# The norm's guard as a 33rd summed value, and two powers in one operation, in a Mamba scan kernel on one core

## The reference

```python
def _layernorm(x, axis=-1, eps=1e-05):
    ...
    return (x - m) / jnp.sqrt(v + eps)
...
xn = x * jax.lax.rsqrt(var + 1e-06) * norm_w        # a second norm, on the layer norm's result
...
def step(h, inp):                                   # h: 8 batches x 256 channels x 16 states
    dA_t, dB_t, x_t, C_t, t = inp
    h = h * dA_t + dB_t * x_t[:, :, None]
    nrm = jnp.sqrt(jnp.sum(h * h, axis=(1, 2), keepdims=True))
    fac = jnp.minimum(20.0 / (nrm + 1e-08), 1.0)
    h = jnp.where(t % 10 == 0, h * fac, h)
    y = jnp.einsum('bdn,bn->bd', h, C_t) + D_param * x_t
    return (h, y)
```

## Time and profile before

| what | us |
|---|---|
| median of 3 runs | 736.2 |
| lowest and highest of them | 733.01, 736.84 |
| span of the profiled execution | 732.8 |
| PE, DVE busy in it | 610.7, 579.2 |
| ACT, POOL busy in it | 581.7, 591.9 |

### The profile page before, as it was taken

How to read it: one execution, slowest core, us unless ns; L and a number is a source line. 1 busy time by engine, 2 the same in 40 slices (tenths; PEclk the granted TensorE clock), 3 DMA queues, 4 the chain that set the end, 5 groups by cost and what they waited for, 6 DMA issues and landing times.

```text
span 732.8 us, 12812 instructions
## 1 busy us (share of the span) xinstructions
PE 610.7 (83%) x3988; PEld 475.9 (65%) x3988; DVE 579.2 (79%) x918; ACT 581.7 (79%) x1218; POOL 591.9 (81%) x567
## 2 busy tenths in 40 slices
PE   6698989889979889998988999898878794289774
PEld 4346667757757667766766766776667783179764
DVE  5577799899889989998998999889898982843221
ACT  4899989999998999999999999999988731233330
POOL 4488889999998989999998999998798860177774
PEclk9889899999989999999999999999988887589998
DMA  5341423245145313614542271244215202147561
GB/s 159 117 157 36 146 80 117 62 143 162 61 145 144 127 63 100 202 61 133 156 127 63 85 210 64 105 139 133 64 66 175 66 18 73 47 129 207 167 182 48
DMA packets 61735, 83.17 MB, mean 114 GB/s; under 512 B 14998, under 2 KB 47544, under 8 KB 61672
## 3 DMA queue, kind: packets, MB, share of 16 engines
q1 hardware_dynamic: 57896, 76.07, 34.0%
q0 software_dynamic: 2560, 6.08, 3.0%
q10 hardware_dynamic: 1216, 0.27, 0.2%
HBM read 69.81 MB, written 12.80 MB: 113 GB/s over the span
## 4 chain that ended last, share of the span: by engine, by line
ACT 27%; PE 22%; issue 17%; POOL 15%; DVE 13%; DMA 4%; POOLq 0%; SPq 0%; DVEq 0%; ACTq 0%
ACT z L1098 9%; POOL h L855 8%; DVE h L1367 7%; PE ps L1725 7%; ACT ps L989 7%; POOL h L869 4%; PE ps L1617 4%; DMA z<-rows_d,gidx 3%; PE ps L588 2%; PE ps L601 2%; ACT L1059 2%; ACT dtb L1059 1%; ACT xx L1016 1%; PE ps L1699 1%; ACT L1098 1%
## 5 line engine op out<-in xcount | busy, mean ns | idle before, releaser
L1367 DVE TENSOR_TENSOR_SCAN h<-ps,h 128x902 f32<-128x902 f32 x204 | 320.4, 1610 | 33.5 <-ACT ps L989 23.6
L855 POOL TENSOR_TENSOR h<-u,scr 128x640 f32<-128x640 f32 x208 | 298.2, 1462 | 2.4
L1725 PEld LDWEIGHTS ps<-h,ident 128*128 128x128 f32 x1632 | 239.4, 199 | 24.2 <-issue 21.8
L1725 PE MATMUL ps<-h,ident 128*128 128x160 f32 x1632 | 243.9, 310 | 3.3 <-issue 3.3
L1098 ACT ACTIVATE z<-dtb,asc 128x240 f32<-128x240 f32 x576 | 237.4, 485 | 0.3
L989 ACT ACTIVATE ps<-z 128x820 f32<-128x820 f32 (+1 forms) x208 | 138.2, 689 | 16.0 <-DVE h L1367 8.9
L869 POOL TENSOR_TENSOR h<-h,scr 128x960 f32<-128x960 f32 (+1 forms) x52 | 106.0, 2038 | 1.1 <-DVE h L1383 1.1
L1418 DVE TENSOR_TENSOR h<-h,ps 128x640 f32<-128x640 f32 (+2 forms) x169 | 106.5, 642 | 0.2
L1617 PE MATMUL ps<-xnT,wT 128*128 128x488 f32 x144 | 77.2, 652 | 0.3 <-ACT xnT L974 0.3
L1699 PE MATMUL ps<-sqb,sel 128*8 128x32 f32 x832 | 33.6, 195 | 37.6 <-ACT sqb L999 27.7
L1699 PEld LDWEIGHTS ps<-sqb,sel 128*8 128x8 f32 x832 | 27.2, 91 | 53.0 <-ACT sqb L999 45.7
(11 more groups left out here) (193 smaller groups left out, 820.2 us busy)
## 6 DMA issues: line engine op xcount, KB each, us to landing
scr<-b_d SPq DMA_DIRECT2D x52, 640.0 KB, 4.6
scr<-c_d SPq DMA_DIRECT2D x52, 240.0 KB, 4.4
z<-in_L_ffn_w_dram SPq DMA_DIRECT2D x32, 256.0 KB, 3.1
cdg<-cdg_d SPq DMA_DIRECT2D x52, 93.8 KB, 2.1
xx_d<-xx SPq DMA_DIRECT2D x8, 256.0 KB, 2.0
xxr<-xx_d SPq DMA_DIRECT2D x8, 256.0 KB, 2.8
rows_d<-h2b SPq DMA_DIRECT2D x16, 120.0 KB, 2.0
rows_d<-xxr SPq DMA_DIRECT2D x16, 120.0 KB, 2.3
```

What stands on the lines that cost most here:

```text
L855: pool.tensor_tensor(o.rearrange("p (n b) t -> p n b t", b=B), us.unsqueeze(1).to_broadcast([P, nn, B, SEG]), bb[:, S % RING, n0 * BS:(n0 ...
L1367: dve.tensor_tensor_scan(hs, region(G)[:, 0:(r1 - r0) * SLOT], hs, 0.0, ALU.mult, ALU.add).then_inc(gscan, 1)
L1725: pe.matmul(ps[:, YB, 0:H * BS], ident[:], hr[:, :, n * B:(n + 1) * B, 0:SEG], start=(n == 0), stop=False)
```

## The change

The guard that POOL added becomes a 33rd value of each batch in `sqb`. It is written once at the start, and PE and DVE sum 33 values where they summed 32. `root` is the power alone, and the semaphore `nrt_done` between its two operations goes. In `ln_pool` the two powers of 4 values each become one of 8, and the product that gives `nmean` moves from part 1 (s = 2) to part 0 (s = 0), into the place of a power; LNK falls from 6 to 5. The squares go to `sqb` with a step of 33 values between batches where it was 32, and the routing logits in PSUM start one value later.

```diff
-LNK = 6
+LNK = 5
+    SQC = H * NST + 1
-        sqb = sb("sqb", [P, ROWS])
+        sqb = sb("sqb", [P, B * SQC])
-        LCOL = NCOL + H * NST
+        LCOL = NCOL + SQC
+        sq_b = sqb[:].rearrange("p (b r) -> p b r", r=SQC)
+        sq_r = sqb[:].rearrange("p (b r) -> p r b", r=SQC)
@@ ln_pool
-                n = [2 * part]
+                n = [(0, 2, 3)[part]]
...
-                    step(pool.tensor_tensor(lnp[:, 0, :], lnp[:, 6, :], neghalf_e[:], ALU.pow))
+                    step(pool.tensor_tensor(nmean, mv[:, :, 0], minus4[:], ALU.mult))
                 elif part == 1:
-                    step(pool.tensor_tensor(lnp[:, 1, :], lnp[:, 7, :], neghalf_e[:], ALU.pow))
-                    step(pool.tensor_tensor(nmean, mv[:, :, 0], minus4[:], ALU.mult))
+                    step(pool.tensor_tensor(lnp[:, 0:2, :], lnp[:, 6:8, :],
+                                            neghalf_e[:].unsqueeze(1).to_broadcast([P, 2, TILES]), ALU.pow))
@@ root
                 pool.wait_ge(s8_ready, k + 1)
-                pool.tensor_tensor(nrm8[:], s8[:], guard8[:], ALU.add).then_inc(nrt_done, 1)
-                pool.wait_ge(nrt_done, k + 1)
-                pool.tensor_tensor(fac8[:], nrm8[:], neghalf_e[0:B, 0:1], ALU.pow).then_inc(rec_done, 1)
+                pool.tensor_tensor(fac8[:], s8[:], neghalf_e[0:B, 0:1], ALU.pow).then_inc(rec_done, 1)
@@ square_last
-                act.activation(sqb[:].rearrange("p (b r) -> p r b", b=B)[:, r0 // B:r1 // B, :],
+                act.activation(sq_r[:, r0 // B:r1 // B, :],
@@ vector engine, start
-            dve.memset(guard8[:], (1e-8 / MAX_NORM) ** 2)
+            dve.memset(sq_b[:, :, H * NST], 1e-8 ** 2 / P)
@@ take_norm
-                dve.tensor_reduce(s8[:], ps[0:B, YB, NCOL:NCOL + H * NST], AX_X, ALU.add).then_inc(s8_ready, 1)
+                dve.tensor_reduce(s8[:], ps[0:B, YB, NCOL:NCOL + SQC], AX_X, ALU.add).then_inc(s8_ready, 1)
@@ norm_sum
-                    ins = pe.matmul(ps[0:B, YB, NCOL:NCOL + H * NST], sel[:, b, :], sqb[:, b * H * NST:(b + 1) * H * NST],
+                    ins = pe.matmul(ps[0:B, YB, NCOL:NCOL + SQC], sel[:, b, :], sq_b[:, b, :],
```

More of the change, by code:

```diff
@@ L105, in mamba_moe @@
         nbias2 = sb("nbias2", [P, TILES])
-        guard8 = sb("guard8", [B, 1])
         neghalf_e = sb("neghalf_e", [P, TILES])
@@ L121, in mamba_moe @@
         cc4 = scr[:, RING * NST * BS:].rearrange("p (r c) -> p r c", r=RING)
-        sqb = sb("sqb", [P, ROWS])
+        sqb = sb("sqb", [P, B * SQC])
         b0s = sb("b0s", [P, B])
         s8 = sb("s8", [B, 1])
-        nrm8 = sb("nrm8", [B, 1])
         fac8 = sb("fac8", [B, 1])
@@ L217, in mamba_moe @@
         s8_ready = sem("s8_ready"); fac_done = sem("fac_done")
-        nrt_done = sem("nrt_done"); rec_done = sem("rec_done")
+        rec_done = sem("rec_done")
         h0_ready = sem("h0_ready"); cb_done = sem("cb_done"); cm_done = sem("cm_done"); cp_done = sem("cp_done")
@@ L1382, in last_step @@
                 dve.wait_ge(bm_done, 4 * NSEG)
-                dve.tensor_tensor(hr[:, :, 1], hr[:, :, 1], sqb[:], ALU.add).then_inc(last_done, 1)
+                dve.tensor_tensor(hr[:, :, 1], hr[:, :, 1], sqb[:, 0:ROWS], ALU.add).then_inc(last_done, 1)
             def last_y():
@@ L1491, in _ @@
             h_first = rows(h, 2)[:, :, 1]
-            dve.tensor_tensor(sqb[:].rearrange("p (b r) -> p r b", b=B), h_first.rearrange("p (r b) -> p r b", b=B),
+            dve.tensor_tensor(sq_r[:, 0:H * NST, :], h_first.rearrange("p (r b) -> p r b", b=B),
                               h_first.rearrange("p (r b) -> p r b", b=B), ALU.mult).then_inc(sq_done, 1)
```

## The result

| | before | after |
|---|---|---|
| median, us | 735.1 (4 runs) | 809.7 (4 runs, 808.05 to 812.38) |
| span of the profiled execution, us | 732.8 | 806.3 |
| DVE, ACT busy, us | 579.2, 581.7 | 654.1, 583.2 |
| POOL, PE busy, us | 591.9, 610.7 | 574.9, 630.9 |

A forecast was written before the change was run, and what follows sets the result against it. ACT was taken to bound the middle windows, PE waiting for `restart` the late stretch. Gains of 2.4 us less 0.1 for the 33rd column gave 2.3 off 736.2: 733.9 us, range 729.6 to 737.3.

The forecast's parts named there:

- the lead: At the shared port, L1324 asks 0.38 us after the power's start, `c_last` 0.51 + 0.15; margin 0.28.
- slower, by the port: Rival: in 16 segments L1324 comes behind `c_last` too, ending 2.2 us later, 1.85 beyond DVE's slack; 765 us, chance 0.03.
- 0.16 us: L1324 on DVE loses this if POOL's power holds the port to its end; nothing if it lets go early.
- 0.26 us of work: In POOL's norm chain, the addition costs 0.26 us by starts: 0.18 in its row, the rest the semaphore to the power.
- the sum: Gains place by place where DVE or PE, not ACT, sets the next scan: together 2.4 us.
- Most middle windows gained nothing: In the middle windows, about 38 segments, an earlier factor only makes scan 2 wait longer for ACT; no gain.
- ACT sets them: In the middle windows ACT bounds the loop, busy for 62.31 of 64.56 us, more than any other engine.
- cover of 0.13 us: In the middle windows scan 2 waits 0.13 us for ACT, which helps cover what L1324 may lose.
- The power of 8 values: In the layer norm on POOL, one power of 8 estimated at 1.65 us, between 1.01 and 2.02.
- The 33rd column: In the norm's sum on PE, 16 rows get 0.02 us longer, on the path in some six segments: 0.1 us lost.
- the squares' step: ACT's squares, written every 132 bytes instead of 128: taken as free; a tenth either way in 50 segments is 1.5 us.

The follow-up runs named there:

- experiment 4: The changed kernel, with POOL waiting for its own power's semaphore before going on to `c_last`; 748.5 us, ratio 0.997 to the kernel before.
- experiment 5: The changed kernel, with an addition of zero into an unused value ahead of the power, no wait between; 826.69 us, ratio 1.104 to the kernel before.
- experiment 7: The kernel before, with the last `c_mult` ahead of `make_xc` on DVE where there is a `make_xc`; 827.56 us, ratio 1.105 to the kernel before.
- experiment 8: The changed kernel, with `make_xc` moved ahead of the second `c_mult` on DVE, right behind the reduction; 746.02 us, ratio 0.996 to the kernel before.
- experiment 3: The changed kernel, with POOL waiting for `make_xc` ahead of `c_last`; 747.56 us, ratio 0.996 to the kernel before; a second time 0.994.
- experiment 6: The changed kernel, with POOL waiting for `c_last`'s own semaphore behind `c_last`; 776.27 us, ratio 1.037 to the kernel before.
- experiment 1: The changed kernel, with an addition of zero and its wait back ahead of the power; 750.07 us, ratio 0.999 to the kernel before.
- experiment 10: The kernel before, with a second addition, of zero, and its wait in the norm's chain; 756.52 us, ratio 1.010 to the kernel before.

## Why the prediction was wrong

**The step that failed** is the lead in the rival "slower, by the port": "L1324 asks 0.38 after the power's start, `c_last` 0.51 + 0.15; the margin is 0.28", and the sentence behind it, that the first to come has it. What isn't so is that POOL's next instruction comes to ask only after its start. Where POOL goes on from the power to `c_last` without a wait, DVE doesn't get in between: the lead over `c_last` was the same in experiments 4 and 5 to 0.03 us, the outcome was 0.65 and 8.59. With that step the forecast's own term fell: for what each L1324 loses behind the power it took 0.16 us, and the changed kernel shows 2.19 in seven places and 7.8 in eight. The forecast took the addition for 0.26 us of work, and left its wait out of the account; because of that wait the power started 0.01 behind `make_xc`, and it was the power that was held up. The Trainium skill (SBUF — State Buffer, SBUF: two separate sides) says that whichever instruction starts first has the port to its end. The runs bear it out where `c_last` already runs as `make_xc` comes (experiment 7) and where `make_xc` runs as the power comes (experiment 8). They don't for the lone power, beside which L1332 and L1326 take 0.65 (experiments 3 and 4), and they don't in the changed kernel, where `make_xc` starts 0.26 ahead of `c_last` and still waits for it: experiments 5 and 6 show that a row of instructions can count as one.

**Its price** was off too, as "2.2 later, 1.85 beyond DVE's slack, in 16 segments: 765" counted `c_last` alone. The seven places of 2.84 are that case. In the eight others POOL had four products behind `c_last` and no pause up to their end, 7.8 us each; so 810 and not 765. (The 16 segments that it counts are 15; S = 0 has two of the 16 operations.) Its chance, 0.03, rested on the margin and on nothing else.

**The 0.16 us** that each L1324 was to lose "if the power holds the port to its end" was nil: 0.65 in experiments 3 and 4. The long power in the earlier trace rows was read as a port held by either side to its end. For this small power it holds only one way: a POOL instruction that finds the port with DVE waits (0.90 in experiment 8, the power 0.40 behind). DVE isn't held up by a small power that stands alone.

**What held.** With the port out of the way, the sum was of the right size: experiment 3 lies 2.5 us under experiment 1, which has the addition back (747.56, 750.07), for 2.4 forecast. By its ratio to the kernel before, 0.996 and 0.994, it is 3 to 4 us. By places the agreement is in part luck. Between the ends of the same scans, the trace of experiment 3 is 1.2 us shorter than that of experiment 1 up to S = 5, where the sum has 0.6, and 2.0 us shorter from the end of window 6 on, where it has 1.4. The windows between them, where it has 0.4 of gain, lost 0.8. Most middle windows gained nothing, as was said: 64.55 us in experiment 3 for 64.56, with `restart` waiting for nothing. DVE's waits for ACT in the scans, from 239 to 500 us, were 10.2 us in 13 before; in the second trace of experiment 3 they are

```profile
DVE h L1375 <- ACT ps L997: 12.6, 21, 1.8
```

That ACT sets them was right, and experiment 10 shows how thin its cover of 0.13 us is. But one window lost 1.3 us, here window 6 in the first trace of experiment 3, which took 64.57 in experiment 1:

```profile
430.56:496.44 65.88, 58.60 (x400) 44.92 (x400) 59.01 (x79) 62.16 (x129) 58.21 (x50) 0.97 0.36 110
```

The second trace of experiment 3 and those of experiments 4 and 8 have one such window each, 65.83 to 65.89, and those of the kernel before and of experiment 1 have none. Its mean clock is 0.97 as in the others; what makes it longer is open. The power of 8 values takes what was estimated, 1.65:

```profile
L815 POOL TENSOR_TENSOR lnp<-lnp,neghalf_e 128x8 f32<-128x8 f32 x8 | 13.2, 1644 | 0.1
```

The 33rd column and the squares' step show in two groups (busy us, mean ns):

```profile
L1700 PE MATMUL ps<-sqb,sel 128*8 128x33 f32 x832 | 36.1, 198 | 32.1 <-ACT sqb L1000 21.4 <-DVE lgb L1442 5.0 <-DVE sqb L1493 4.9
```

```profile
L1000 ACT ACTIVATE sqb<-h 128x48 f32<-128x48 f32 x51 | 14.9, 292 | 7.3 <-DVE h L1368 2.6
```

198 ns a matmul (195 before), and 292 a square for 289 before: no cost that a run can tell, as experiment 1 says of all of them.

**Left open.** Whether POOL holds the port while it has a next instruction ready, or asks for the next one's sake while the last still runs, no run tells apart; both give these numbers. How short a pause may be wasn't tried: all here are 0.08 us or longer. L811 in s = 5 and L858 in s = 0 both start 0.03 before `c_last` ends, and DVE slips in ahead of the first and not of the second; experiment 7 has the same (2.37 and 8.00). The second `make_xc` of S = 0 even gets in between two products, in the changed kernel as it does behind `c_last` in the earlier trace rows:

```profile
51.60 4.73 POOL L858 TENSOR_TENSOR h<-u,scr 128x640 f32<-128x640 f32 x3
...
52.35 1.24 DVE L1325 SCALAR_TENSOR_TENSOR xc<-thx,xc 128x488 f32<-128x488 f32 x1
```

So with a pause in POOL's row `make_xc` never waited beyond it here, and without one POOL kept the port in all places but these. What makes the difference there is open.

## What to carry to other kernels

Before taking a small instruction off GpSimd, look at what VectorE does beside it: if an operation with two SBUF inputs starts there, the wait behind the small one may be its only way to the port. Price such a collision at up to all that GpSimd issues before its next pause, not by the next instruction alone. Where the two must be close, give VectorE the start by an order of its own, or set one wait on GpSimd ahead of its long work; here either turned 10% slower into 0.3 to 0.6% faster.

## What the runs showed of the hardware

- GpSimd can keep the port that it shares with VectorE over instructions that follow each other without a pause: a VectorE operation of 0.65 us took 8.47, behind `c_last` and four products, although it had started 0.26 us ahead of `c_last`. It ended 0.52 to 0.53 us behind the last of them, each time.
- A pause of 0.08 us on GpSimd, from waiting for its own last instruction, breaks such a row: ahead of `c_last` it left the VectorE operation at its plain 0.65 us (experiment 4), behind `c_last` it brought 8.47 down to 2.84 (experiment 6).
- A GpSimd power of one value on 8 partitions, with a wait behind it, didn't hold up the VectorE operation that started 0.24 us behind it (0.65), while one that started 0.15 us behind such an operation took 0.90 for 0.53.
- With one of its two inputs in PSUM, the same VectorE operation runs beside GpSimd's `c_last` in its plain 0.65 us.
